# Softmax of a sparse graph-attention layer: exponentials per head with bias and accumulated sum on ScalarE

## The chip, the cores and the metric

The kernel runs on one core of one Trainium2 chip, as one launch. The metric is the device time of that launch in microseconds (us). A core has five engines, each with its own in-order queue: TensorE (PE, with its weight loads shown as PEld), VectorE (DVE), ScalarE (ACT), GpSimd (POOL) and SyncE (SP, which only starts transfers). They wait for each other through semaphores. Sixteen DMA engines are shared by all queues.

## The reference

One graph attention layer over 8192 nodes with 8 heads of width 32, in fp32. After a layer norm and a ReLU:

```python
h = (x @ W.T).reshape(n, H, D)                       # n=8192, H=8, D=32
s_src = einsum('nhd,hd->nh', h, a_src); s_dst = einsum('nhd,hd->nh', h, a_dst)
attn = s_src[:, None, :] + s_dst[None, :, :]
attn = attn + adj[:, :, None] * We[:, 0] + be
attn = where(adj > 0, attn, -inf)                    # only the edges count
attn = leaky_relu(attn, 0.2); attn = softmax(attn, axis=1)
out = einsum('ijh,jhd->ihd', attn, h) + x @ Wr.T + br + x0     # x0: the layer's input
```

`adj` is 8192 x 8192 fp32, some 268 MB, with few non-zero entries per row: most in the first rows, few in the last. So a row's softmax runs over its edges only.

## The kernel before

**Stages.** A prologue (to about 209 us) norms and projects all rows and writes a table of (h, s_dst) rows to HBM. The sparse stage then works through 63 tiles of 128 rows, and the epilogue (from about 2370 us) does tile 0, whose rows have too many edges, densely.

**Sparse stage, in two streams.** A *find* (`find`, `sort_step`, `decode`; sources c0 to c62, one tile of `adj` each) takes the edges out of a dense 128 x 8192 tile: DVE scans it with MAX8 (L615) and FIND_INDEX8 (L619) and sorts what it found in alternating steps. A *unit* (u0 to u62) is 128 rows with lists of at most K edges each. K falls from 75 (u0) over 36 (u7) and 22 (u10) to 6 (u62), with a rise at the start of each group of 8 tiles; within a group the rows are dealt out by their number of edges, so that rows of like length share a unit. For a unit:

- POOL gathers K table rows per partition, one indirect DMA for each (L493), into a ring of 86 slots.
- ACT makes the edge part of the scores in `prepare` (L932, 8 instructions, one for each head).
- DVE does the softmax in `softmax_step`, with its steps m = 0 to 6 between the sort steps of the find of that time: m=0 adds the gathered s_dst (L728), m=1 is the leaky ReLU (L732), m=2 the maximum of each head (L736), m=3 subtracts it (L739), m=5 sums the exponentials (L743), m=6 takes the reciprocal (L746).
- ACT takes the exponentials of all heads in one instruction (L942, `exps`), then weights the last 3 to 16 slots, 8 copies with a scale each (L947). DVE weights the others (`weight`, L755). PE adds the slots up with identity matmuls (L1079 for DVE's, L1085 for ACT's). DVE divides (`evacuate`, L765) one unit later, and POOL adds the result to `out` (L502) three units later.

**What orders it.** The queues are written out in Python. DVE's order for a unit is: the find, the sort steps with the softmax steps between, `weight`, `decode`, `evacuate` of the unit before. ACT's order is `prepare(u+1)`, `exps(u)` with its copies, `prepare(u+2)` and so on. `found[u]` says how many finds are done by unit u: 4, 7, 10, 12, 15, 16, 18, 20 for u0 to u7, then one for each unit until u50 does the last, c62.

SP loads the `adj` tiles (L394) into two buffers, eight pieces of 512 KB for each tile. The load of tile c waits for the scan of tile c-2 (semaphore `scanned`), and from tile 16 on each piece also waits until the piece before has landed, so that one piece at a time is under way.

For each of the groups there is a ranking: DVE counts (`count`, L685 to L696), PE sums in `ranks` (L1096 to L1103, queued behind `tile_sums` of the same unit, and so behind ACT's last copy of that unit), and DVE picks the ranks up one unit later in `place` (L705 to L715), which waits for PE. Then POOL deals the lists out (L512) before it goes on gathering. The rankings that matter below are those of u4 (picked up in u5), u10 (in u11) and u50 (in u51).

Of the kernel before, what the change touches and what calls it, by code (L numbers as in the profile page):

```python
# [15 lines left out]
ALU = mybir.AluOpType  # L16
ACT = mybir.ActivationFunctionType
# [3 lines left out]
AX_X = mybir.AxisListType.X  # L21

P = 128
N = 8192
IN = 256
H = 8
# [144 lines left out]
def gat_kernel(nc, x, adj, W, We, be, a_src, a_dst, Wr, br, out):  # L171
# [4 lines left out]
    with ExitStack() as ctx:  # L176
# [3 lines left out]
        def sb(name, shape, dt=F32):  # L180
            return ctx.enter_context(nc.sbuf_tensor(name, shape, dt))
# [66 lines left out]
        pre = sb("pre", [P, 2, KMAX * H])  # L248
        prob = sb("prob", [P, 2, KMAX * H])
        flag8 = sb("flag8", [P, 1])  # L250
        rmax = sb("rmax", [P, H])
        rsum = sb("rsum", [P, H])
        rinv = sb("rinv", [P, 2, H])
        w_flat = w_all[:, :, :].rearrange("p c n -> p (c n)")
        out_sb = w_flat[:, 0:OUTS * HD].rearrange("p (b n) -> p b n", n=HD)
# [6 lines left out]
        def part(width):  # L262
# [42 lines left out]
            "dec", "decoded", "pre_done", "flag_a", "flag_b",  # L305
            "headed", "validated", "counted", "compared", "above_summed", "rank_ps", "rank_picked", "rank_added", "ranked",
            "over_a", "over_b", "over_c",
            "landed0", "landed1", "landed2", "landed3", "z1", "z2", "z3", "z_ready", "exped", "summed_p", "recip",
            "weighted", "part_sum", "tile_sum", "evac",
            "fl_t", "fl_max", "fl_row", "fl_ready", "gr_ready", "act_weighted", "flag_init",  # L310
            "d_adj", "d_free", "d_mask", "d_ot", "d_oT", "d_dst0", "d_dst1", "d_w", "d_h0", "d_h1", "d_acc", "d_u1", "d_m1", "d_m2", "d_m", "d_leak", "d_own", "d_src", "d_exp",
# [19 lines left out]
        def landed(eng, seq):  # L331

            for lane in range(LANES):
                if seq > lane:
                    eng.wait_ge(S[f"landed{lane}"], 16 * ((seq - lane + LANES - 1) // LANES))
# [207 lines left out]
        def _(dve):  # L543
            v = nc.vector
# [173 lines left out]
            def softmax_step(un, m):  # L718

                u, K, b = un.u, un.K, un.u % 2  # L720
                z, pr = pre[:, b, 0:K * H], prob[:, b, 0:K * H]
                zv = z.rearrange("p (k h) -> p k h", h=H)
                zh, prh = (w.rearrange("p (k h) -> p h k", h=H) for w in (z, pr))
                if m == 0:
                    landed(dve, un.gather_seq + K)
                    dve.wait_ge(S["pre_done"], u + 1)
                    for k, at, n in un.slots(0, K):
                        last = v.tensor_tensor(zv[:, k:k + n, :], zv[:, k:k + n, :], gath[:, at:at + n, HD:ROW], ALU.add)  # L728
                    last.then_inc(S["z1"], 1)
                elif m == 1:  # L730
                    dve.wait_ge(S["z1"], u + 1)
                    v.scalar_tensor_tensor(out=z, in0=z, scalar=ALPHA, in1=z, op0=ALU.mult, op1=ALU.max  # L732
                                           ).then_inc(S["z2"], 1)
                elif m == 2:
                    dve.wait_ge(S["z2"], u + 1)
                    v.tensor_reduce(rmax[:, :], zh, AX_X, ALU.max).then_inc(S["z3"], 1)  # L736
                elif m == 3:
                    dve.wait_ge(S["z3"], u + 1)
                    v.tensor_tensor(zv, zv, rmax[:, :].unsqueeze(1).to_broadcast([P, K, H]), ALU.subtract  # L739
                                    ).then_inc(S["z_ready"], 1)  # L740
                elif m == 5:
                    dve.wait_ge(S["exped"], u + 1)
                    v.tensor_reduce(rsum[:, :], prh, AX_X, ALU.add).then_inc(S["summed_p"], 1)  # L743
                elif m == 6:
                    dve.wait_ge(S["summed_p"], u + 1)
                    v.reciprocal(rinv[:, b, :], rsum[:, :]).then_inc(S["recip"], 1)  # L746

            def weight(un):
# [136 lines left out]
        def _(act):  # L885
            s = nc.scalar
# [49 lines left out]
            def exps(un):  # L936

                u, K, b = un.u, un.K, un.u % 2
                act.wait_ge(S["z_ready"], u + 1)
                if u >= 2:  # L940
                    act.wait_ge(S["act_weighted"], units[u - 1].act_before)
                s.activation(prob[:, b, 0:K * H], pre[:, b, 0:K * H], ACT.Exp).then_inc(S["exped"], 1)  # L942
                act.wait_ge(S["exped"], u + 1)
                for k in range(K - un.act_slots, K):
                    for h in range(H):
                        g = gath[:, un.slot(k), h * D:(h + 1) * D]
                        last = s.activation(g, g, ACT.Copy, scale=prob[:, b, k * H + h:k * H + h + 1])  # L947
                    last.then_inc(S["act_weighted"], 1)

            prepare(units[0])  # L950
            for un in units:
                if un.u + 1 < len(units):
                    prepare(units[un.u + 1])
                exps(un)
# [248 lines left out]
```

## Time and profile before

| | us |
|---|---|
| median of 3 runs (2674.48 to 2684.55) | 2684.43 |
| the profiled execution, its own time | 2684.95 |
| span of that execution in the trace | 2683.3 |
| DVE busy | 2132.3 |
| POOL busy | 1485.7 |
| ACT busy | 1246.5 |
| PE busy | 1235.0 |

The profiled execution's own time is 1.65 us above its span, which is what lies around the trace. A row of the timeline gives the start, the duration, the engine, the line and the operation, the shapes, and in brackets how long the engine had sat idle before and what ended that. A row xN is N instructions that follow each other. The chain of waits is followed back from the last instruction, at each step to what released it. The granted TensorE clock is 0.681 of full speed on average.

### The profile page before, as it was taken

How to read it: one execution, taken by the hardware profiler on the slowest of the kernel's cores; microseconds unless marked ns; L12 is line 12 of the kernel's file. 1: busy time of each engine (PE TensorE's matmuls, PEld its weight loads, DVE VectorE, ACT ScalarE, POOL GpSimd, SP SyncE). 2: the span in 40 equal slices, each digit the busy share in tenths (PEclk: the TensorE clock that was granted, in tenths of full speed). 3: DMA queues.
4: the chain of work that ended last, by engine and by line, in shares of the span. 5: the costliest groups of instructions: out<-in, count | busy, mean ns of one | idle time of the engine just before them, and what ended most of it. 6: DMA issues, size and time to landing. Idle time of an engine off the chain costs nothing.

```text
span 2683.3 us, 27007 instructions
## 1 busy us (share of the span) xinstructions
PE 1235.0 (46%) x5305; PEld 934.2 (35%) x5306; DVE 2132.3 (79%) x4852; ACT 1246.5 (46%) x4898; POOL 1485.7 (55%) x1666
## 2 busy tenths in 40 slices
PE   6990022503334367446424524533341453518885
PEld 4660022402324245334322512422241342416664
DVE  3448959998998898999889988988997841259992
ACT  2320030221245498667546546444542655826662
POOL 5772656756675777777777476277347437710000
PEclk9995556757666676666666666666665666759998
DMA  3665656686676877877777677678668614477660
GB/s 114 195 228 191 216 131 195 167 249 178 179 226 192 225 240 225 245 229 243 229 224 239 199 233 222 183 231 233 208 193 234 200 39 100 95 225 173 157 156 3
DMA packets 226527, 512.79 MB, mean 191 GB/s; under 512 B 98280, under 2 KB 116400, under 8 KB 224208
## 3 DMA queue, kind: packets, MB, share of 16 engines
q1 hardware_dynamic: 151280, 319.60, 37.2%
q0 software_dynamic: 74960, 191.61, 28.1%
q14 instruction: 110, 0.90, 0.1%
q8 instruction: 33, 0.54, 0.1%
q10 hardware_dynamic: 144, 0.13, 0.0%
HBM read 475.19 MB, written 36.03 MB: 191 GB/s over the span
## 4 chain that ended last, share of the span: by engine, by line
DMA 56%; issue 18%; PE 10%; DVE 6%; POOL 6%; ACT 2%; SPq 1%; POOLq 0%; DVEq 0%; ACTq 0%; PEldq 0%
DMA adj_sb<-in_adj_dram 40%; DMA arena<-table,arena 8%; DMA arena<-table,own 6%; POOL arena L493 5%; PE banks L1058 2%; PE banks L1052 2%; ACT arena L947 1%; PE banks L1101 1%; DVE work L619 1%; PE banks L1079 1%; DVE work L615 1%; PE banks L1055 1%; PE banks L1154 1%; PE banks L1144 1%; DMA out_dram<-w_all,arena 1%
## 5 line engine op out<-in xcount | busy, mean ns | idle before, releaser
L493 POOL DMA_INDIRECT arena<-table,arena x943 | 972.6, 1031 | 354.5 <-issue 231.2
L1079 PE MATMUL banks<-arena,ident 128*128 128x256 f32 x1268 | 426.9, 513 | 1142.1 <-DVE arena L755 1142.1
L947 ACT ACTIVATE arena<-arena,prob 128x32 f32<-128x32 f32 x4024 | 859.5, 306 | 2.1
L1079 PEld LDWEIGHTS banks<-arena,ident 128*128 128x128 f32 x1268 | 332.6, 268 | 1234.8 <-issue 984.6
L615 DVE MAX8 work<-adj_sb 128x8 f32<-128x184 f32 (+51 forms) x624 | 580.9, 1005 | 116.0 <-DMA adj_sb<-in_adj_dram 115.5
L619 DVE FIND_INDEX8 work<-work,adj_sb 128x8 uint32<-128x184 f32 (+51 forms) x624 | 618.6, 1013 | 0.0
L942 ACT ACTIVATE prob<-pre 128x104 f32<-128x104 f32 (+26 forms) x63 | 20.3, 322 | 965.6 <-DVE pre L739 965.6
L1085 PE MATMUL banks<-arena,ident 128*128 128x256 f32 x1006 | 312.6, 442 | 106.3 <-ACT arena L947 106.2
L493 POOL DMA_INDIRECT arena<-table,own x194 | 202.2, 1042 | 157.4 <-DMA arena<-table,own 55.6
L1085 PEld LDWEIGHTS banks<-arena,ident 128*128 128x128 f32 x1006 | 197.3, 212 | 209.0 <-ACT arena L947 188.5
L932 ACT ACTIVATE pre<-arena,we_all 128x13 f32<-128x13 f32 (+23 forms) x480 | 146.5, 400 | 80.1 <-DMA arena<-lists 80.1
L755 DVE TENSOR_TENSOR arena<-arena,prob 128x768 f32<-128x768 f32 (+7 forms) x158 | 183.3, 1209 | 0.0
L502 POOL DMA_INDIRECT out_dram<-w_all,arena x60 | 99.7, 1662 | 147.3 <-DVE w_all L765 101.2
L728 DVE TENSOR_TENSOR pre<-pre,arena 128x80 f32<-128x80 f32 (+20 forms) x76 | 19.6, 271 | 165.9 <-DMA arena<-table,arena 131.8
L512 POOL DMA_INDIRECT lists<-arena,rank x60 | 59.7, 996 | 141.0 <-DVE rank L712 119.7
L1101 PE MATMUL banks<-work,ones 128*128 128x24 f32 (+6 forms) x404 | 89.1, 375 | 0.0
L1101 PEld LDWEIGHTS banks<-work,ones 128*128 128x128 f32 x404 | 85.6, 312 | 0.0
L1154 PE MATMUL banks<-ident,adj_sb 128*128 128x128 f32 x256 | 45.1, 308 | 62.4 <-ACT adj_sb L975 62.4
L1144 PE MATMUL banks<-pre,work 128*32 128x128 f32 x512 | 73.4, 290 | 0.0
L1058 PE MATMUL banks<-w_all,arena 128*128 128x256 f32 x256 | 72.4, 405 | 0.0
L1052 PE MATMUL banks<-w_all,arena 128*128 128x272 f32 x256 | 70.1, 397 | 0.0
L836 DVE TENSOR_TENSOR arena<-arena 128x4096 f32<-128x4096 f32 x16 | 70.0, 4419 | 0.0
(140 smaller groups left out, 1789.2 us busy)
## 6 DMA issues: line engine op xcount, KB each, us to landing
adj_sb<-in_adj_dram SPq DMA_DIRECT2D x504, 512.0 KB, 4.0
arena<-dst_rows SPq DMA_DIRECT2D x16, 2048.0 KB, 8.5
arena<-table,arena POOLq DMA_INDIRECT x943, 3.5
table<-arena POOLq DMA_DIRECT2D x32, 264.0 KB, 2.9
arena<-in_x_dram SPq DMA_DIRECT2D x32, 256.0 KB, 3.0
resid<-arena POOLq DMA_DIRECT2D x32, 256.0 KB, 2.6
out_dram<-arena POOLq DMA_DIRECT2D x32, 256.0 KB, 2.8
work<-table SPq DMA_DIRECT2D x8, 1024.0 KB, 10.9
```

Source lines behind the costliest of these rows:

```text
L493: pool.indirect_dma_start(gath[:, un.slot(k), :], None, table[:, :], bass.IndirectOffsetOnAxis(ap=rec[:, k, 0:1], axis=0), bounds_check=N ...
L615: last = v.max(val8[:, 8 * s:8 * s + 8], a[:, bounds[s]:bounds[s + 1]])
L619: last = v.max_index(idx8[:, 8 * s:8 * s + 8], val8[:, 8 * s:8 * s + 8], a[:, bounds[s]:bounds[s + 1]])
L755: last = v.tensor_tensor(gv, gv, pb.unsqueeze(3).to_broadcast([P, n, H, D]), ALU.mult)
L932: last = s.activation(pv[:, h, :], pairs(rec, K)[:, :, 1], ACT.Identity, scale=we_all[:, h:h + 1], bias=rec[:, 1 + h:2 + h])
L947: last = s.activation(g, g, ACT.Copy, scale=prob[:, b, k * H + h:k * H + h + 1])
L1052: m.matmul(ps_hd[:, q, b, :], rows, w_all[:, c, 0:272], start=(c == 0), stop=(c == 1))
L1058: last = m.matmul(ps_res[:, q, b, :], rows, w_all[:, c, 272:528], start=(c == 0), stop=(c == 1))
L1079: last = m.matmul(ps_sum[:, u % 2, :], ident[:, :], gath[:, un.slot(k), 0:HD], start=(k == 0), stop=False)
L1085: last = m.matmul(ps_sum[:, u % 2, :], ident[:, :], gath[:, un.slot(k), 0:HD], start=False, stop=(k == K - 1))
L1101: m.matmul(rv[:, i, :], ones[:, :], same[:, j * D:(j + 1) * D], start=False, stop=(i == n - 1 and j == i - 1))
L1144: last = m.matmul(ps_acc[:, b, :], hv[:, 4 * q + r, :], pt_sb[q % 4][:, r * P:(r + 1) * P], start=(q == 0 and r == 0), stop=(q == 15 and r ...
```

## The change

`rneg` (128 x 8) is new. Step m=3 no longer subtracts the maximum from all K x 8 scores: it negates the 8 maxima. ScalarE takes the exponentials head by head, with that head's negated maximum as bias (a pointer operand of one value for each partition) and with the sum over the head as accumulated output into `rsum`; the signal `exped` comes with the last head. Step m=5 (the sum) is gone with its semaphore, and the reciprocal at m=6 waits for `exped`.

```diff
@@ softmax_step
                 elif m == 3:
                     dve.wait_ge(S["z3"], u + 1)
-                    v.tensor_tensor(zv, zv, rmax[:, :].unsqueeze(1).to_broadcast([P, K, H]), ALU.subtract
-                                    ).then_inc(S["z_ready"], 1)
-                elif m == 5:
+                    v.tensor_scalar(rneg[:, :], rmax[:, :], -1.0, None, ALU.mult).then_inc(S["z_ready"], 1)
+                elif m == 6:
                     dve.wait_ge(S["exped"], u + 1)
-                    v.tensor_reduce(rsum[:, :], prh, AX_X, ALU.add).then_inc(S["summed_p"], 1)
-                elif m == 6:
-                    dve.wait_ge(S["summed_p"], u + 1)
                     v.reciprocal(rinv[:, b, :], rsum[:, :]).then_inc(S["recip"], 1)
@@ exps
-                s.activation(prob[:, b, 0:K * H], pre[:, b, 0:K * H], ACT.Exp).then_inc(S["exped"], 1)
+                ph, zh = (w[:, b, 0:K * H].rearrange("p (k h) -> p h k", h=H) for w in (prob, pre))
+                for h in range(H):
+                    last = s.activation(ph[:, h, :], zh[:, h, :], ACT.Exp, bias=rneg[:, h:h + 1], accum_out=rsum[:, h:h + 1])
+                last.then_inc(S["exped"], 1)
```

DVE's queue around the softmax of unit u50 (K = 11), before: the rows from the maximum to the first weighting; MAX and MATCH_REPLACE are the sort steps of find c62.

```order
L736 TENSOR_REDUCE rmax<-pre 128x8 [waits z2]
L651 MATCH_REPLACE work<-work 128x56 [waits sorted_]
L652 MATCH_REPLACE work<-work 128x56
L739 TENSOR_TENSOR pre<-pre,rmax 128x88 [waits z3]
L648 MAX work<-work 128x8 [waits sorted_]
L649 MAX work<-work 128x8
L654 TENSOR_SCALAR ahi<-work 128x20 [waits sorted_]
L743 TENSOR_REDUCE rsum<-prob 128x8 [waits exped]
L746 RECIPROCAL rinv<-rsum 128x8 [waits summed_p]
L755 TENSOR_TENSOR arena<-arena,prob 128x3x256 [waits exped]
```

The same place of the changed kernel (its line numbers differ by a few):

```order
L737 TENSOR_REDUCE rmax<-pre 128x8 [waits z2]
L652 MATCH_REPLACE work<-work 128x56 [waits sorted_]
L653 MATCH_REPLACE work<-work 128x56
L740 TENSOR_SCALAR rneg<-rmax 128x8 [waits z3]
L649 MAX work<-work 128x8 [waits sorted_]
L650 MAX work<-work 128x8
L655 TENSOR_SCALAR ahi<-work 128x20 [waits sorted_]
L743 RECIPROCAL rinv<-rsum 128x8 [waits exped]
L752 TENSOR_TENSOR arena<-arena,prob 128x3x256 [waits exped]
```

The subtraction over 88 columns has become an operation on 8, the sum is gone, and the reciprocal is now the first that waits for ScalarE.

ScalarE's queue at units u9 and u10 (K = 24 and 22), before:

```order
L942 ACTIVATE prob<-pre 128x192
L947 ACTIVATE arena<-arena,prob 128x32 x112
L932 ACTIVATE pre<-arena,we_all 128x20 x8
L942 ACTIVATE prob<-pre 128x176
L947 ACTIVATE arena<-arena,prob 128x32 x112
```

And now:

```order
L941 ACTIVATE prob,rsum<-pre,rneg 128x24 x8
L947 ACTIVATE arena<-arena,prob 128x32 x112
L929 ACTIVATE pre<-arena,we_all 128x20 x8
L941 ACTIVATE prob,rsum<-pre,rneg 128x22 x8
L947 ACTIVATE arena<-arena,prob 128x32 x112
```

One exponential of K x 8 columns has become eight of K columns; nothing else moved on this engine.

## Rows read from the trace of the kernel before

**Rows 1.** The page: the chain that ended last, share of the span by lines.
```profile
DMA adj_sb<-in_adj_dram 40%; DMA arena<-table,arena 8%; DMA arena<-table,own 6%; POOL arena L493 5%; PE banks L1058 2%; PE banks L1052 2%; ACT arena L947 1%; PE banks L1101 1%; DVE work L619 1%; PE banks L1079 1%; DVE work L615 1%; PE banks L1055 1%; PE banks L1154 1%; PE banks L1144 1%; DMA out_dram<-w_all,arena 1%
```

**Rows 2.** Who waited for whom: us in total, times, longest.
```profile
ACT prob L942 <- DVE pre L739: 965.6, 58, 99.2
...
DVE work L615 <- DMA adj_sb<-in_adj_dram: 115.5, 32, 9.0
...
DVE work L705 <- PE banks L1103: 25.3, 3, 9.6
...
DVE rsum L743 <- ACT prob L942: 22.2, 13, 8.3
```

**Rows 3.** The same view for SP's queue.
```profile
SPq L394 <- DMA adj_sb<-in_adj_dram: 1243.2, 336, 7.3
SPq L394 <- DVE work L619: 498.5, 17, 76.4
```

**Rows 4.** The chain of waits between 1100 and 2142 us, by lines.
```profile
by line: DMA adj_sb<-in_adj_dram 98.5%; SPq L394 1.1%; issue 0.6%
```

**Rows 5.** Groups of instructions: count, busy us, mean ns, idle us before.
```profile
L947 ACT ACTIVATE arena<-arena,prob 128x32 f32<-128x32 f32 x4024 | 859.5, 306 | 2.1
...
L743 DVE TENSOR_REDUCE rsum<-prob 128x8 f32<-128x104 f32 (+26 forms) x63 | 25.5, 405 | 22.2 <-ACT prob L942 22.2
...
L739 DVE TENSOR_TENSOR pre<-pre,rmax 128x104 f32<-128x104 f32 (+26 forms) x63 | 19.0, 301 | 0.4
```

**Rows 6.** Timeline of ACT in the dense epilogue, an exponential with accumulated sum.
```profile
2440.91 3.70 ACT L975 ACTIVATE arena<-arena,nmax 128x4096 f32<-128x4096 f32 x1
2444.51 0.19 ACT L975 ACTIVATION_READ_ACCUMULATOR arena<-arena,nmax 128x1 f32 x1
2444.60 0.25 ACT L980 ACTIVATE ot_sb<-banks 32x128 f32<-32x128 f32 x1
```

**Rows 7.** Timeline of ACT at unit u4 (K = 32).
```profile
770.97 0.42 ACT L942 ACTIVATE prob<-pre 128x256 f32<-128x256 f32 x1 [71.20 <-DVE pre L739]
771.42 27.23 ACT L947 ACTIVATE arena<-arena,prob 128x32 f32<-128x32 f32 x128
```

**Rows 8.** Timeline of DVE at unit u9 (K = 24).
```profile
983.92 0.35 DVE L739 TENSOR_TENSOR pre<-pre,rmax 128x192 f32<-128x192 f32 x1
...
985.68 0.18 DVE L746 RECIPROCAL rinv<-rsum 128x8 f32<-128x8 f32 x1
```

**Rows 9.** Timeline of ACT, the exponentials of u8, u9 and u10.
```profile
956.14 0.38 ACT L942 ACTIVATE prob<-pre 128x208 f32<-128x208 f32 x1 [0.56 <-DVE pre L739]
...
984.31 0.36 ACT L942 ACTIVATE prob<-pre 128x192 f32<-128x192 f32 x1 [1.53 <-DVE pre L739]
...
1011.91 0.35 ACT L942 ACTIVATE prob<-pre 128x176 f32<-128x176 f32 x1 [0.98 <-DVE pre L739]
```

**Rows 10.** The chain of waits around the load of tile c26: start, us, what.
```profile
1064.55 9.79 DVE work L619 x10
...
1074.36 3.77 DMA adj_sb<-in_adj_dram
```

**Rows 11.** Timeline of POOL, the first deal of the last group.
```profile
2192.63 1.02 POOL L512 DMA_INDIRECT lists<-arena,rank  x1 [19.29 <-DVE rank L712]
```

**Rows 12.** Timeline of ACT, the exponentials of u50, u56, u59, u60, u61 and u62.
```profile
2167.66 0.28 ACT L942 ACTIVATE prob<-pre 128x88 f32<-128x88 f32 x1 [14.79 <-DVE pre L739]
...
2285.41 0.27 ACT L942 ACTIVATE prob<-pre 128x104 f32<-128x104 f32 x1
...
2323.44 0.26 ACT L942 ACTIVATE prob<-pre 128x72 f32<-128x72 f32 x1 [3.02 <-DVE pre L739]
...
2336.16 0.26 ACT L942 ACTIVATE prob<-pre 128x64 f32<-128x64 f32 x1 [3.27 <-DVE pre L739]
...
2347.09 0.25 ACT L942 ACTIVATE prob<-pre 128x56 f32<-128x56 f32 x1 [1.50 <-DVE pre L739]
...
2357.89 0.24 ACT L942 ACTIVATE prob<-pre 128x48 f32<-128x48 f32 x1 [5.32 <-DVE pre L739]
```

More of the change, by code:

```diff
@@ L252, in gat_kernel @@
         rsum = sb("rsum", [P, H])
+        rneg = sb("rneg", [P, H])
         rinv = sb("rinv", [P, 2, H])
@@ L307, in gat_kernel @@
             "over_a", "over_b", "over_c",
-            "landed0", "landed1", "landed2", "landed3", "z1", "z2", "z3", "z_ready", "exped", "summed_p", "recip",
+            "landed0", "landed1", "landed2", "landed3", "z1", "z2", "z3", "z_ready", "exped", "recip",
             "weighted", "part_sum", "tile_sum", "evac",
@@ L720, in softmax_step @@
                 u, K, b = un.u, un.K, un.u % 2
-                z, pr = pre[:, b, 0:K * H], prob[:, b, 0:K * H]
+                z = pre[:, b, 0:K * H]
                 zv = z.rearrange("p (k h) -> p k h", h=H)
-                zh, prh = (w.rearrange("p (k h) -> p h k", h=H) for w in (z, pr))
+                zh = z.rearrange("p (k h) -> p h k", h=H)
                 if m == 0:
```

## The prediction

> **What bounds the kernel now.** I read four views, in this order. First the chain that ended last, by lines: the loads of the `adj` tiles are 40% of it, every compute line a few per cent [rows 1]. Then SP's waits: it waited 336 times for an `adj` piece to land (1243.2 us), but only 17 times for DVE's scan [rows 3]. Then the same chain between 1100 and 2142 us: 98.5% of it is `adj` pieces, one behind the other [rows 4]. So in that stretch, 1042 us long and u13 to u49 of the units, neither DVE nor ACT sets the time, although DVE is busy for 2132.3 us of the span. DVE itself waits for an `adj` tile 32 times, 115.5 us, 3.6 us each [rows 2]. Last the waits between the engines. ACT's exponentials waited 58 times for L739 (965.6 us), so ACT is mostly idle when they come. DVE waited only 22.2 us for them, because sort steps stand between. And three times DVE waited in L705 for PE's ranks (25.3 us) [rows 2], which themselves stand behind ACT's last copy of that unit. The reader should see that a change to the softmax is paid only where DVE or ACT is last: before tile c26 is loaded, and after c62 has been scanned.
>
> **What goes and what comes.** On DVE L739 (mean 0.30 us) and L743 (mean 0.41) go, 19.0 + 25.5 = 44.5 us in 63 units [rows 5]. A negation of 8 columns comes. The trace has none; the nearest row is the reciprocal of 8 columns, 0.18 us [rows 8], so 11 us. DVE's busy time falls by 33 us.
>
> On ACT one instruction becomes eight exponentials and eight reads of the accumulator. The nearest row to a short exponential with one pointer operand is the copy with a scale: 0.306 us for 32 columns [rows 5], and 128 of them take 27.23 us, 0.213 each from start to start [rows 7], so each begins 0.093 before the last one ends. 32 columns cost 0.027 of that: from 256 columns (0.42) to 88 (0.28) is 0.83 ns a column [rows 7, 12]. The read of the accumulator takes 0.19, starts 0.09 before its exponential ends, and the next instruction starts 0.09 after the read [rows 6]. A head of K columns is then 0.186 + 0.00083 K for the exponential and 0.095 for the read, and eight heads are 2.25 + 0.0066 K, plus 0.09 for the end of the last: 2.50 us for K = 24, 2.41 for K = 11. Bounds: if the reads cost nothing, 0.76 us less for a unit; if nothing overlaps, 0.49 a head, 1.6 us more. I take the overlapped value, since the epilogue's own pair of instructions shows it; its length there is another (4096 columns), which is why both bounds stay in the range.
>
> The cover: before, the exponential (0.3 to 0.4) ran under the two sort steps at m=4 and m=5. In u9, L739 begins at 983.92 and L746 at 985.68, 1.76 us later [rows 8]. Afterwards the reciprocal comes at 0.18 + 0.03 + 2.50 + 0.04 = 2.75: **DVE gets 1.0 us longer in this unit, not shorter**. With the shorter sorts of K < 16 it is 1.6 us longer. ACT's last head ends later by 2.50 - 0.36 - (0.35 - 0.18) = 1.97 us [rows 8, 9]. What is queued behind: on DVE `weight`, `decode` and the next find; on ACT the copies and with them PE's sums and ranks.
>
> **Where it counts.** I add up the delay along the chain.
>
> 1. Start to c16. The gathers of u0 to u3 end last there, not the softmax; u0 has so many sort steps that its sum goes for free (-0.2). u3 adds 0.3 on DVE. In u4 (K = 32) eight heads take 2.55 instead of 0.42, less 0.23 for the shorter step: +1.9. ACT's 128 copies follow without a pause [rows 7], then PE's ranks, then L705 in u5, where DVE waits (it is one of the three waits of rows 2). So the find of c16 is late by **2.0**, and its scan starts the load of c18.
>
> 2. c19 to c26. The loads carry the 2.0 to c19. u7 ends its heads 1.9 later: 3.9. Now ACT is nearly full: before the exponentials of u8, u9 and u10 it was idle for 0.56, 1.53 and 0.98 us only [rows 9], with 112 copies and eight `prepare` instructions between, and each unit adds 2.14. u8: 3.9 - 0.56 + 2.14 = 5.5. u9: the scores come later than ACT is free, 4.3, + 2.14 = 6.4. u10: 6.4 - 0.98 + 2.14 = 7.6. Behind u10's copies stand PE's ranks, behind these L705, the find of c24, and its scan ends at 1074.34, from where the load of c26 starts 0.02 later [rows 10]. Late by 7.6: **+5.6** in this step.
>
> 3. c26 to c62, 1074 to 2146 us: the loads follow each other [rows 4], and a find that is late by less than its wait costs nothing. DVE's growth of 1.0 to 1.6 us a unit stands against 3.6 us of wait a tile. Up to 1280 us the cover is thin, since there DVE hardly waits: in seven units it falls some 6 us further behind than the loads already are, and whether SP is by then still busy with the tile before is all that covers it. **0**, but this is the term most likely to be wrong upwards.
>
> 4. u50. Its exponentials (0.28 at 2167.66) are followed by copies, PE's ranks, L705, and POOL, which sat idle 19.29 us for this [rows 11, 12] and then paces the tail with its gathers: 2.41 - 0.28 - 0.06 = **+2.1**.
>
> 5. u55 to u62. POOL's gathers go on at their pace. ACT has no idle time before u56 [rows 12], nor before u57 and u58, and adds 2.15 in each: 2.0, 4.1, 6.3, 8.4. Then its idle 3.02, 3.27, 1.50 and 5.32 before u59 to u62 [rows 12] take some back: 8.4 - 3.0 + 2.1 = 7.5, 6.4, 7.0, and 7.0 - 5.3 + 2.1 = **3.8** for u62, whose copies, sum and store the epilogue waits for. The epilogue has none of the edited lines.
>
> Sum: 2.0 + 5.6 + 0 + 2.1 + 3.8 = 13.5 us. On the profiled execution (2684.95) that gives 2698.5. That execution lies 0.5 above the median of the runs, so the median should come to 2684.4 + 13.5 = 2698.0.
>
> **A rule of the skill.** The epilogue's rows give the read of the accumulator 0.19 us, of which 0.095 shows [rows 6]. The Trainium skill, "ScalarE: Activation LUTs", section "What ACT_TABLE_LOAD costs", prices an ACTIVATE with one pointer operand at 280 ns + 0.833 ns a column, with 93 ns of overlap back to back, and names no read at all; an estimate by that page alone makes eight heads 1.66 us for K = 11, and the sum about 3 us. The trace agrees with the page on the ACTIVATE and shows the read beside it.
>
> **The rivals.**
>
> - *The reads hide.* If an accumulator read runs wholly under the next exponential, a unit is 0.76 us shorter on ACT. Step 1 is then 1.0, step 2 about 0.5 (ACT stays below its idle time), steps 4 and 5 are 1.3 and 1.3, less 1 where DVE gains: about +3, 2687.5. Against it: L980 did wait for the read [rows 6]. 10%.
> - *The loads swallow step 2 as well*, because c25's pieces or SP's order leave more room than one execution shows: 2.0 + 2.1 + 3.8 = +8, 2692. For it: SP waited for a scan only 17 times. Against: c26 is one of these [rows 10]. 12%.
> - *Short instructions don't overlap with the read.* 1.6 us more a unit: steps 1 and 4 +1.6 each, step 2 +6, step 5 up to +12, and step 3 opens, since DVE's growth of 3 us a unit finds no cover in eight units before 1280 us, +24. About +59, 2743; with half of it +25, 2710. It decides from about 0.32 us a head. 14%.
> - *Faster: DVE is the bound and the cover suffices.* If eight heads took no longer than the sort steps (1.6 us and less), each unit on DVE's chain would save 0.30 + 0.41 - 0.18 = 0.53 us; about nine are on it (u3, u4, u7 to u11, u50, u62): -5, 2680. It needs under 0.18 us a head, and even the copies take 0.213 [rows 7]. 4%.
> - *The edit doesn't do what it says*, for instance a table load for each head: the instruction order shows one load of the table, before u0, as before, and no instruction beside the eight. Left out.
>
> **How the numbers follow.** The forecast (2693 to 2706, around 2698.0) has 60%. A measurement of this kernel can tell about 0.5%, 13.4 us, from no change: the limit is 2697.9, in the middle of my forecast. Of the 60% a little over half lies above, since what can go wrong in step 3 goes up; with the 14% that is 0.50 slower. Faster by more than 0.5% (below 2671) needs more than the rival gives; 0.03 for it and for the spread of the runs, of which one was at 2674.48. The rest, 0.47, is within. The range leaves out the lowest and the highest tenth: 2686 to 2714.
>
> **What the profile would show.** Right: eight exponentials and eight reads of a unit in 2.4 to 2.5 us; L746's successor waiting for ACT in nearly all units, over 50 us in all; DVE's busy time 33 us down and ACT's 130 up; the scan of c24 ending about 7.6 us later and that of c62 too; u62's heads ending 13.5 later. Wrong in step 3 if SP waits for scans between 1100 and 2142 us; wrong in step 2 if the scan of c24 moves by 2 or by 15; wrong in price if eight heads take 1.7 or 3.9 us.

## The result, and the profile after

The changed kernel takes **2700.77 us** (median of 9 runs, 2689.68 to 2703.26), the kernel before 2683.01 us beside it (9 runs, 2674.48 to 2691.09). The ratio is 1.0058, 95% interval 1.0038 to 1.0077: slower by 15 to 18 us, depending on whether the ratio or the two medians are taken. The profiled execution has a span of 2700.6 us, 17.3 more than before, at a granted clock of 0.680 (0.681 before).

The page of the changed kernel, busy time of each engine:

```profile
PE 1242.3 (46%) x5305; PEld 927.9 (34%) x5306; DVE 2106.1 (78%) x4789; ACT 1387.8 (51%) x5843; POOL 1483.3 (55%) x1666
```

DVE is busy for 26 us less than before, ACT for 141 us more. The groups of instructions of the changed kernel (count, busy us, mean ns, idle us before and what ended it) show from what:

```profile
L941 ACT ACTIVATE prob<-pre,rneg 128x13 f32<-128x13 f32 (+26 forms) x504 | 156.4, 313 | 845.6 <-DVE rneg L740 845.5
L941 ACT ACTIVATION_READ_ACCUMULATOR prob<-pre,rneg 128x1 f32 x504 | 94.1, 187 | 0.0
```
```profile
L743 DVE RECIPROCAL rinv<-rsum 128x8 f32<-128x8 f32 x63 | 12.8, 203 | 181.5 <-ACT prob L941 181.5
L740 DVE TENSOR_SCALAR rneg<-rmax 128x8 f32<-128x8 f32 x63 | 11.5, 183 | 0.4
```

504 exponentials and 504 reads of the accumulator stand where 63 exponentials stood. The negation costs what was assumed, 11.5 us. The last column of the reciprocal is the new thing: DVE waits for ACT in all 63 units, 181.5 us, where the sum had waited 22.2 us [rows 2]. Who waited for whom on DVE and on SP's queue, changed kernel (us in total, times, longest):

```profile
DVE rinv L743 <- ACT prob L941: 181.5, 63, 12.8
...
DVE work L616 <- DMA adj_sb<-in_adj_dram: 55.3, 20, 8.0
...
DVE work L706 <- PE banks L1103: 22.5, 3, 9.0
```
```profile
SPq L395 <- DMA adj_sb<-in_adj_dram: 1246.6, 336, 6.5
SPq L395 <- DVE work L620: 507.2, 17, 76.8
```

These answer rows 2 and 3. DVE's waits for an `adj` tile went from 115.5 us in 32 tiles to 55.3 us in 20: the 60 us that vanished there are what the longer units were paid with. SP still waits for a scan only 17 times, as before. And the chain of waits of the stretch in which the loads follow each other [rows 4] is as it was:

```profile
by line: DMA adj_sb<-in_adj_dram 98.7%; SPq L395 1.1%; issue 0.6%
```

The timeline of ACT at unit u9 (K = 24; start, duration, and in brackets the idle time before) shows the price of a head:

```profile
986.79 0.34 ACT L941 ACTIVATE prob<-pre,rneg 128x24 f32<-128x24 f32 x1 [0.36 <-DVE rneg L740]
987.03 0.19 ACT L941 ACTIVATION_READ_ACCUMULATOR prob<-pre,rneg 128x1 f32 x1
987.12 0.32 ACT L941 ACTIVATE prob<-pre,rneg 128x24 f32<-128x24 f32 x1
...
989.26 0.18 ACT L941 ACTIVATION_READ_ACCUMULATOR prob<-pre,rneg 128x1 f32 x1
989.48 1.17 ACT L947 ACTIVATE arena<-arena,prob 128x32 f32<-128x32 f32 x5
```

From one head to the next are 0.32 us, of which the read shows 0.09. From 986.79 to the end of the last read are 2.66 us; before, one instruction of 0.36 [rows 9]. DVE in the same unit:

```profile
986.54 0.22 DVE L740 TENSOR_SCALAR rneg<-rmax 128x8 f32<-128x8 f32 x1
...
989.48 0.20 DVE L743 RECIPROCAL rinv<-rsum 128x8 f32<-128x8 f32 x1 [1.52 <-ACT prob L941]
```

From this step to the reciprocal are 2.94 us against 1.76 [rows 8], and 1.52 of it is waiting. So DVE's unit is longer by 1.2 us although two of its instructions are gone.

Where the 17.3 us of the two traces lie, by events that both have:

| from | to | before | after | more | forecast |
|---|---|---|---|---|---|
| start | scan of c16 ends | 837.2 | 838.8 | 1.6 | 2.0 |
| start | scan of c24 ends | 1074.3 | 1080.3 | 5.9 | 7.6 |
| load of c26 issued | load of c62 issued | 1040.8 | 1045.0 | 4.2 | 0 |
| scan of c62 | heads of u50 end | 3.2 | 5.3 | 2.1 | 2.1 |
| first add of u53 | heads of u62 end | 142.2 | 145.9 | 3.8 | 3.8 |
| heads of u62 end | end | 325.2 | 327.6 | 2.4 | 0 |

These pieces don't cover the whole span; what lies between them (the end of c62's load and scan, u50 to u53) changed by -1.1 us together. The differences are taken before rounding.

### The profile page after: what moved, and what is told of

Same layout as the page of the kernel before. It is cut to its first block, busy times and chain, and to the rows that moved or that the text cites. A ratio compares the mean times of both kernels' runs of the same rounds, so it can differ in the third digit from the quotient of the medians.

```text
span 2700.6 us, 27889 instructions
## 1 busy us (share of the span) xinstructions
PE 1242.3 (46%) x5305; PEld 927.9 (34%) x5306; DVE 2106.1 (78%) x4789; ACT 1387.8 (51%) x5843; POOL 1483.3 (55%) x1666
## 4 chain that ended last, share of the span: by engine, by line
DMA 53%; issue 16%; PE 10%; DVE 9%; ACT 5%; POOL 5%; SPq 1%; POOLq 0%; DVEq 0%; ACTq 0%; PEldq 0%
DMA adj_sb<-in_adj_dram 40%; DMA arena<-table,arena 6%; DMA arena<-table,own 5%; POOL arena L494 4%; ACT arena L947 4%; DVE work L620 2%; PE banks L1058 2%; DVE work L616 2%; PE banks L1052 2%; PE banks L1101 1%; PE banks L1055 1%; PE banks L1154 1%; PE banks L1144 1%; ACT prob L941 1%; DVE adj_sb L822 1%
## 5 line engine op out<-in xcount | busy, mean ns | idle before, releaser
L1079 PEld LDWEIGHTS banks<-arena,ident 128*128 128x128 f32 x1268 | 323.3, 261 | 1214.3 <-issue 967.3
L616 DVE MAX8 work<-adj_sb 128x8 f32<-128x184 f32 (+51 forms) x624 | 580.9, 1006 | 56.1 <-DMA adj_sb<-in_adj_dram 55.3
L941 ACT ACTIVATE prob<-pre,rneg 128x13 f32<-128x13 f32 (+26 forms) x504 | 156.4, 313 | 845.6 <-DVE rneg L740 845.5
L494 POOL DMA_INDIRECT arena<-table,own x194 | 202.0, 1041 | 155.5 <-DMA arena<-table,own 55.3
L1085 PEld LDWEIGHTS banks<-arena,ident 128*128 128x128 f32 x1006 | 198.7, 217 | 249.7 <-ACT arena L947 230.2
L743 DVE RECIPROCAL rinv<-rsum 128x8 f32<-128x8 f32 x63 | 12.8, 203 | 181.5 <-ACT prob L941 181.5
L941 ACT ACTIVATION_READ_ACCUMULATOR prob<-pre,rneg 128x1 f32 x504 | 94.1, 187 | 0.0
```

Of the source, the lines that this page charges most:

```text
L494: pool.indirect_dma_start(gath[:, un.slot(k), :], None, table[:, :], bass.IndirectOffsetOnAxis(ap=rec[:, k, 0:1], axis=0), bounds_check=N ...
L616: last = v.max(val8[:, 8 * s:8 * s + 8], a[:, bounds[s]:bounds[s + 1]])
L941: last = s.activation(ph[:, h, :], zh[:, h, :], ACT.Exp, bias=rneg[:, h:h + 1], accum_out=rsum[:, h:h + 1])
L1079: last = m.matmul(ps_sum[:, u % 2, :], ident[:, :], gath[:, un.slot(k), 0:HD], start=(k == 0), stop=False)
L1085: last = m.matmul(ps_sum[:, u % 2, :], ident[:, :], gath[:, un.slot(k), 0:HD], start=False, stop=(k == K - 1))
```

## The experiments

Theory: the new instructions take ACT some 2.1 to 2.3 us more a unit, this counts only before c26 is loaded (part A) and after c62 is scanned (part B), and in between the loads of `adj` hide it (part C). The rivals that the prediction named lay in the price of a head (reads that hide, or heads that don't overlap), in the loads swallowing part A, and in DVE being the bound. Runs of one lot share the runs of the kernel before: its medians were 2689.67, 2688.03 and 2683.1 us in the three lots.

### One stretch of units at a time

The softmax of the changed kernel for some units, that of the kernel before for the others; both forms and both waits stand in the same program.

```diff
+        new = lambda u: u <= 12              # e1; e2: 13 <= u <= 49; e3: u >= 50
...
+                if new(u):
+                    for h in range(H):
+                        last = s.activation(ph[:, h, :], zh[:, h, :], ACT.Exp, bias=rneg[:, h:h + 1], accum_out=rsum[:, h:h + 1])
+                else:
+                    last = s.activation(prob[:, b, 0:K * H], pre[:, b, 0:K * H], ACT.Exp)
```

Expected of u0 to u12 alone:

> The change in u0 to u12 only; all other units as in the kernel before. My theory (the path runs through u4's copies, the ranks, c16, then u7 to u10, the ranks, c24, and SP then goes on from there): the whole early part of the sum stays, +6 to +8 us, and the scan of c24 ends 6 us later than before, as in the kernel after. Rival (the adj loads swallow it, since their chain has room): 0 to +2 us at the end, although DVE and ACT are as late in these units.

Expected of u13 to u49 alone:

> The change in u13 to u49 only, 37 of 63 units, in which it adds 1.0 to 1.6 us each to DVE and 2 us each to ACT. Theory (the loads of the adj tiles, one piece at a time, set the time there): 0 to +3 us; DVE's waits for adj tiles shrink from 115 us to some 55 us. Rival (DVE sets the time there after all): +37 to +60 us. Second rival (the softmax of this stretch slows the pieces themselves by contention, which would be the 4 us by which the load chain from c26 to c62 grew in the kernel after): +4 to +6 us, with the load chain from c26 to c62 at 1045 us and not 1041.

Expected of u50 to u62 alone:

> The change in u50 to u62 only. Theory: +2.1 us through u50's copies, the ranks and the deal, and +3.8 us through ACT, which has no idle time in u55 to u58: +6 us, with the heads of u62 ending 5.9 us later. Rival (POOL's gathers alone pace the tail): +2 us.

| changed units | median us | ratio, 95% | in us | forecast |
|---|---|---|---|---|
| u0 to u12 | 2698.07 | 1.0035 [1.0021, 1.0049] | +9.4 (5.6 to 13.2) | 7.6 |
| u13 to u49 | 2688.88 | 0.9998 [0.9982, 1.0014] | -0.5 (-4.8 to 3.8) | 0 |
| u50 to u62 | 2694.85 | 1.0022 [1.0007, 1.0037] | +5.9 (1.9 to 10.0) | 5.9 |

The three ratios add up to 0.55%, the whole change has 0.58%. **The loss is made in 26 of the 63 units, and the 37 in the middle cost nothing that these runs can show.** The intervals of the single rows are wide, though: 9.4 against 7.6 or against the +6 to +8 us expected is no difference that they can tell. The rival in which the loads swallow the second step asked for 2 us from the first row, and the row's interval begins at 5.6.

That the middle units are not cheap but covered is in DVE's waits of the second kernel (u13 to u49 changed):

```profile
DVE rinv L757 <- ACT prob L956: 74.6, 37, 3.3
DVE work L619 <- DMA adj_sb<-in_adj_dram: 56.5, 21, 9.1
```

and in those of the first (u0 to u12 changed):

```profile
DVE work L619 <- DMA adj_sb<-in_adj_dram: 116.1, 32, 8.0
```

In the middle DVE waits 74.6 us for ACT, 37 times, and in exchange 60 us less for `adj`. The tail is reproduced as closely: with u50 to u62 changed, first add of u53 to the last head of u62 takes 146.1 us, with the change in all units 145.9, with it in the others alone 142.6 and 142.5, before 142.2.

The same three traces say something about the 4.2 us of the middle stretch. From the load of c26 to that of c62 they have 1046.5, 1043.6 and 1050.4 us; the largest stands in the kernel in which none of these units is changed. So this length moves by some 10 us from one execution to the next without the edit, and the 4.2 us can't be put down to it.

### What of a head costs how much

First the kernel before with eight exponentials and nothing else: no bias, no accumulated sum, DVE subtracts and sums as before.

```diff
-                s.activation(prob[:, b, 0:K * H], pre[:, b, 0:K * H], ACT.Exp).then_inc(S["exped"], 1)
+                for h in range(H):
+                    last = s.activation(ph[:, h, :], zh[:, h, :], ACT.Exp)
+                last.then_inc(S["exped"], 1)
```

> The kernel before with its one exponential taken head by head in eight instructions; DVE still subtracts and sums, no bias operand, no accumulated sum. It separates the price of eight instructions from that of the pointer operand and the reads. Theory (fixed price by operand: about 0.11 us a head from start to start without a pointer and without a read): eight heads in 1.0 to 1.1 us, mostly under the sort steps, +2 to +4 us in all. Rival (an instruction of ScalarE costs 0.19 us a head whatever its operands): 1.6 us, +7 us.

Then the changed kernel without `accum_out`; DVE sums again at m=5.

```diff
-                    last = s.activation(ph[:, h, :], zh[:, h, :], ACT.Exp, bias=rneg[:, h:h + 1], accum_out=rsum[:, h:h + 1])
+                    last = s.activation(ph[:, h, :], zh[:, h, :], ACT.Exp, bias=rneg[:, h:h + 1])
```

> The changed kernel without the accumulated output: ScalarE still takes eight exponentials with the negated maximum as bias, VectorE sums them as before (behind the last head). It takes the eight reads of the accumulator away and gives DVE its 0.41 us sum back. Theory (a read shows 0.095 us): eight heads 0.76 us shorter than in the kernel after, 1.75 to 1.9 us; the stretch from the find of c19 to the end of c24's scan takes 3 to 4 us more than before (after: 6.3), the tail from the scores of u53 to the last head of u62 1 to 2 us more (after: 3.9); in all +7 us on before. Rival (the reads hide under the next exponential): both stretches as in the kernel after and +15 to +18 us.

The timeline of ACT at u9 (K = 24), the eight heads of the first kernel and of the second:

```profile
986.94 1.18 ACT L944 ACTIVATE prob<-pre 128x24 f32<-128x24 f32 x8 [1.25 <-DVE pre L739]
```
```profile
990.23 1.92 ACT L945 ACTIVATE prob<-pre,rneg 128x24 f32<-128x24 f32 x8 [1.06 <-DVE rneg L740]
```

| eight heads, us | K = 24 | K = 13 |
|---|---|---|
| one instruction (before) | 0.36 | 0.29 |
| eight exponentials | 1.18 | 1.02 |
| with the bias as pointer | 1.92 | 1.77 |
| with the read as well (after) | 2.66 | 2.51 |

So the price has three layers of nearly the same size: splitting 0.8 us, the bias 0.74 (0.093 an instruction), the read 0.74 (0.093). Rival "the reads hide" asked for 0.76 less than the forecast heads, that is 1.74 for K = 24; it is excluded. So is "short instructions don't overlap" with 3.9, and so is the rival of the first of these two kernels (0.19 us a head whatever the operands), which asked for 1.6 where 1.18 was measured.

The Trainium skill, "ScalarE: Activation LUTs", section "What ACT_TABLE_LOAD costs", adds about 93 ns for each pointer operand of an ACTIVATE: the two kernels agree with it, 0.093. It names no price for the read, which shows another 0.093 here.

In time: eight exponentials alone 2694.74 us, ratio 1.0025 [1.0007, 1.0043], +6.7 (1.9 to 11.6); with the bias 2699.94, 1.0039 [1.0026, 1.0053], +10.5 (7.0 to 14.2); the whole change about +15.6 by its ratio. Both medians lie above what was expected (+2 to +4, and +7), the first where its rival put it (+7). The time alone doesn't decide between the two; the eight heads do. The intervals overlap, but the order is that of the price, and the stretch from the find of c19 to the scan of c24, in which DVE waits for no load behind the first, has the same order, in us: 172.0 before, 174.6, 176.8, 178.2. The tail from the first add of u53 to the last head of u62 has 142.2, 142.3, 143.3 and 145.9.

### DVE's saving alone

The subtraction and the sum left out, the negation left in, one exponential as before; the softmax of this kernel is then not normalised, so it computes something else, and its time shows what DVE's saving is worth at most.

```diff
-                    v.tensor_tensor(zv, zv, rmax[:, :].unsqueeze(1).to_broadcast([P, K, H]), ALU.subtract
-                                    ).then_inc(S["z_ready"], 1)
-                elif m == 5:
-                    dve.wait_ge(S["exped"], u + 1)
-                    v.tensor_reduce(rsum[:, :], prh, AX_X, ALU.add).then_inc(S["summed_p"], 1)
+                    v.tensor_scalar(rsum[:, :], rmax[:, :], -1.0, None, ALU.mult).then_inc(S["z_ready"], 1)
```

> Only what VectorE is spared, at no price on ScalarE: the kernel before without the subtraction and without the sum (one exponential on the scores as they are, the negated maxima stand in the place of the sums). Its outputs are not the reference's. Theory (DVE is on the path only before c26, in u0 and from u50 on): -4 to -8 us although 44.5 us of DVE's work are gone; DVE's waits for adj tiles grow from 116 us to some 140 us. Rival (DVE, busy 79% of the span, is the bound): -30 to -40 us.

2683.8 against 2688.03 us, ratio 0.9982 [0.9968, 0.9996]: 4.8 us (1.1 to 8.6), within a few tenths of the prediction's rival "faster" (-5). DVE is busy for 2103.8 us, 28.5 less than before. Of that 11.9 us turn up as more waiting for `adj` (115.5 before; 140 had been expected), and 7.6 as more waiting for ACT's exponential, for which there are now fewer instructions in between (22.2 before):

```profile
DVE work L615 <- DMA adj_sb<-in_adj_dram: 127.4, 35, 9.4
...
DVE rinv L742 <- ACT prob L938: 29.8, 14, 8.9
```

An engine that is busy for 79% of the span gives back some 5 of 28 us, at most 9. That is the reading of rows 1 to 4, measured.

### Take the cover away: larger `adj` pieces

If the middle units are only hidden by the loads, quicker loads must bring their price to light. `PIECES = 4` makes four pieces of 1 MB out of eight of 512 KB, in the kernel before and in the changed one.

```diff
-PIECES = 8
+PIECES = 4
```

The kernel before with it:

> The kernel before with the adj tiles loaded in 4 pieces of 1 MB and not in 8 of 512 KB, still one piece at a time. Theory (from c26 to c62 the landings of the pieces in a row set the time, 29 us a tile for 8 pieces of 3.6 us; fewer pieces mean fewer times the fixed part of a landing): the chain from c26's to c62's load, 1041 us before, falls to 960 to 1000 us and DVE's waits for adj tiles fall under 30 us; -40 to -80 us. Rival (bandwidth, not the landing, sets a piece's time): within 10 us of before.

The changed kernel with it:

> The kernel after with the same 4 pieces. Theory: with the loads no longer last, DVE is, and its growth of 1.0 to 1.6 us in each of u13 to u49 comes on the path: +40 to +60 us against the same 4 pieces with the softmax of before, where with 8 pieces the difference was 18 us. Rival (the units of the middle cost nothing whatever the loads do): +15 to +20 us against it.

The kernel before falls to 2622.45 us, ratio 0.9733 [0.9707, 0.9758]; the changed one to 2678.02, 0.9961 [0.9949, 0.9974]. **The gap between the two softmaxes grows from some 16 us to 56 or 61** (2678.02 - 2622.45 gives 55.6, the ratios 2.28%; the two profiled executions are 45.7 apart). Why the loads are quicker, from the page's DMA issues (count, size, median us from issue to landing), first of the kernel before, then with four pieces:

```profile
adj_sb<-in_adj_dram SPq DMA_DIRECT2D x504, 512.0 KB, 4.0
```
```profile
adj_sb<-in_adj_dram SPq DMA_DIRECT2D x252, 1024.0 KB, 5.4
```

Twice the bytes cost 1.4 us more. If a piece costs a fixed part and a part in proportion to its bytes, which two sizes can't show, the fixed part is an estimated 2.6 us. SP waits for the piece before at 7 of the 8 pieces of a tile, and at 3 of 4: the first piece of a tile asks only for the scan, so it is issued while the last of the tile before is still under way, and two pieces are in flight there. That is why a tile of the kernel before took 1040.8 / 36 = 28.9 us in this stretch and not 8 x 4.0. SP's waits in the kernel before with four pieces:

```profile
SPq L394 <- DVE work L619: 1042.5, 61, 79.4
SPq L394 <- DMA adj_sb<-in_adj_dram: 743.1, 144, 7.9
```

The 144 waits for a piece are 3 in each of 48 tiles and take 743.1 us, where 336 (7 a tile) took 1243.2 [rows 3]. And now all 61 loads that can wait for a scan do so, against 17. DVE waits for `adj` in the middle no more, and is busy for 895.5 of the 950 us between 1100 and 2050, where it was 846.8. The chain of waits in this stretch has left the loads, but it is not DVE's alone; it goes back and forth between DVE and POOL's gathers (kernel before with four pieces):

```profile
by line: DMA arena<-table,arena 33.8%; issue 21.9%; POOL arena L493 11.1%; DVE work L619 7.0%; DVE work L615 6.6%; DMA out_dram<-w_all,arena 6.4%; DMA lists<-arena,rank 3.1%; ACT arena L947 1.8%; DVE arena L755 1.2%; POOL lists L512 1.0%; P
```

POOL in turn waits for DVE's ranks, the more the later DVE is; its waits in the same stretch, kernel before with four pieces, then the changed one:

```profile
POOL lists L512 <- DVE rank L712: 26.0, 2, 18.7
```
```profile
POOL lists L513 <- DVE rank L713: 63.3, 3, 26.6
```

DVE's waits between 1100 and 2050 us, kernel before with four pieces, then the changed one:

```profile
DVE pre L728 <- DMA arena<-table,arena: 40.0, 3, 18.7
DVE pre L728 <- issue: 5.8, 3, 4.0
DVE rsum L743 <- ACT prob L942: 1.3, 2, 0.8
```
```profile
DVE rinv L743 <- ACT prob L941: 70.9, 34, 3.6
DVE pre L729 <- DMA arena<-table,arena: 19.6, 1, 19.6
```

69.6 us more of waiting for ACT, 26 less for gathers (a later DVE finds them landed), some 15 less of work for as many units: 28 net; the stretch from the load of c26 to that of c62 grew by 35.5 (973.5 to 1009.0). So the mechanism is there, with its size to a fifth; the kernel with four pieces and the change in the middle alone, below, has 1011.2 us there. This is the stretch that the prediction priced at nothing and called most likely to be wrong upwards; it is nothing only as long as the tiles come as slowly as they do in eight pieces.

### Give DVE work to do while ACT takes the heads

Three kernels that look for a better version. First the change in u13 to u49 alone on four pieces; then the same with three of the next find's MAX8 (about 0.7 us each) put ahead of the reciprocal, where DVE stands idle.

```diff
+                    if m == 6 and new(un.u) and c is not None and c + 1 < len(sources):
+                        find_head(c + 1, 3)
                     softmax_step(un, m)
```

> 4 pieces for each adj tile, and the change in u13 to u49 only. With 8 pieces the same edit measured 0. Theory (with 4 pieces DVE, not the loads, sets the time of this stretch): 37 units of 1.0 to 1.4 us = +35 to +50 us against the kernel before with 4 pieces (2622 us), so 2655 to 2675. Rival (the 56 us between the two kernels with 4 pieces came from the ends, u0 to u12 and u50 on): +0 to +10 us, 2622 to 2632.

> As the kernel with 4 pieces and the change in u13 to u49, but VectorE takes the first three MAX8 of the next tile's find before the reciprocal, where it would wait for the eight heads; nothing else is moved or left out. Theory (the price of the change on DVE is the uncovered wait, 1.9 of 2.4 us): the wait goes to 0.1 to 0.3 us a unit, and each unit is then 0.3 to 0.5 us shorter than with the softmax of before: -10 to -20 us against the kernel before with 4 pieces, 2602 to 2612. Rival (ScalarE's longer work delays the sums and the gathers in another way): no better than 2650.

Without cover 2669.53 us, ratio 0.9947 [0.993, 0.9964]; with it 2628.15, 0.9784 [0.9752, 0.9816]. **The cover gives back 41 us of what the middle units cost on four pieces.** That cost is some 57 us by the ratios (0.9947 against 0.9733), which are of two lots. The traces have it in the stretch itself, from the scan of c24 to that of c62: 1023.8 us with the softmax of before, 1065.7 with the change in the middle units, 1025.0 with the cover, so that 40.7 of 41.9 us come back. This is the strongest evidence that the wait at the reciprocal, and not ACT's busy time as such, was the price: ACT does just as much in both. But it is no better than the softmax of before, where 10 to 20 us better had been expected; by its ratio (0.9784 against 0.9733, of two lots, with intervals that just meet) it may be worse. DVE's waits between 1100 and 2050 us in the kernel with cover say why:

```profile
DVE pre L743 <- DMA arena<-table,arena: 38.3, 3, 20.8
DVE rinv L768 <- ACT prob L969: 16.3, 21, 3.6
```

What DVE saves in 35 units there is 9.4 us of subtractions and 12.3 of sums less 6.3 of negations, 15.4 us; and the cover is too short in 21 units, which takes 16.3 us. In this stretch the two cancel. Whether a longer cover would gain anything is open: DVE waits 38.3 us for gathers there too, and the gathers and POOL's instructions that issue them are 51% of the chain of waits of this stretch.

Last, eight pieces for the 16 densest tiles and four after, with the softmax of before, and with the middle units changed and covered:

```diff
-PIECES = 8
+PIECES = lambda t: 8 if t < 16 else 4
```

> The kernel before with 8 pieces for the tiles up to 15, whose pieces do not wait for each other, and 4 from tile 16 on. With 4 pieces everywhere the scores of u3 came 12 us later than before (688.5 for 676.0 us), while the loads of that stretch are not on the path. Theory (bigger pieces in flight together slow the gathers of u0 to u3): 5 to 12 us better than 4 pieces everywhere, 2610 to 2618. Rival (that shift is the spread of the runs): 2618 to 2628.

> All together: 8 pieces up to tile 15 and 4 from there, the change in u13 to u49 with three MAX8 as its cover, and the softmax of before in the other units, where ScalarE is on the path. Theory: the sum of its parts, 15 to 30 us better than 4 pieces alone, 2592 to 2607. Rival (with DVE faster, POOL's gathers, 1.3 us each, become last in the middle): 2605 to 2622.

2613.59 us, ratio 0.9733 [0.9702, 0.9763], and 2615.95, 0.9746 [0.9711, 0.978]. By its ratio the first is not distinguishable from four pieces everywhere; that the early tiles like smaller pieces is therefore not shown. The second misses what was expected of it (2592 to 2607) and lies where its rival put it (2605 to 2622), whose reason the chain of waits between 1100 and 2050 us supports in part: gathers and the instructions that issue them are 49% of it, 41% with the softmax of before. The two kernels differ by less than their runs do. Both beat the kernel before by 2.5 to 2.7%: **what gains is the larger pieces; the change adds nothing to them, covered or not, and costs 56 us uncovered.**

## Why the prediction was right

**The sum.** Forecast 2698.0 us, measured 2700.77; +13.5 against +15.6 by the ratio (10.2 to 20.7) and +17.3 in the traces. What the traces have beyond the sum is 4.2 us in the load chain and 2.4 in the epilogue, both of which vary as much in kernels that don't touch them (the epilogue's last stretch had 324.0 to 327.6 us over all of them), less 1.7 by which steps 1 and 2 were too large and 1.1 between the pieces of the table. So where the loss is made, and by what, was right; that the total agrees to 2 or 4 us is in part luck, since the spread of these two stretches alone is larger.

**The price of a head.** Forecast 2.50 us for K = 24 and 2.41 for K = 11; measured 2.66, and 2.51 for K = 13. The overlap and the read (0.095 forecast, 0.093 measured) were right. The column was not: from K = 13 to 24 the eight heads grow by 0.15 us, 1.7 ns for each column of a head, twice the 0.83 taken from instructions with adjacent columns. A head's columns lie 8 elements apart, in what it reads and in what it writes. The writing alone is not it: the instructions of `prepare` also write 8 elements apart but read every second element, and eight of them take 2.42 us for K = 13 and 2.50 for K = 24, about 1 ns a column. That leaves the reading 8 apart as the likely cause, but no run changed it by itself. In u9 the heads were 0.16 us longer than forecast, which is most of the 1.2 us more on DVE instead of 1.0.

**Step 1** (start to c16, +2.0): 1.6. u4's heads ended 1.6 late, forecast 1.9.

**Step 2** (to the scan of c24, +5.6, in all 7.6): in all 5.9. Its entry was off, "The loads carry the 2.0 to c19. u7 ends its heads 1.9 later: 3.9". The find of c19 began at 902.04 instead of 902.28, and u7 ended 2.0 late. DVE's first scan instruction of c19, in the kernel before, in the changed one, and in the kernel with the change in u0 to u12:

```profile
902.28 9.17 DVE L615 MAX8 work<-adj_sb 128x8 f32<-128x101 f32 x9 [9.02 <-DMA adj_sb<-in_adj_dram]
```
```profile
902.04 9.17 DVE L616 MAX8 work<-adj_sb 128x8 f32<-128x101 f32 x9 [6.05 <-DMA adj_sb<-in_adj_dram]
```
```profile
905.87 9.17 DVE L619 MAX8 work<-adj_sb 128x8 f32<-128x101 f32 x9 [5.76 <-DMA adj_sb<-in_adj_dram]
```

The loads of c18 and c19 start with the end of the scan of c16 and do carry its delay, but how long they take varies: from that scan to the find of c19 were 65.1 us before, 63.3 in the changed kernel, 63.0 in the third, and 62.5 to 65.1 in the kernels that change other things. The kernel before stands at the long end, so 1.6 late became 0.2 early, and in the third kernel 5.7 late became 3.6. (Those 5.7 us are no measure of step 1: 4.1 of them were there in the heads of u3 beyond the changed kernel's, which has the same softmax up to there.) From the entry on the forecast adds 3.7 up to the scan of c24, and the trace 3.9: heads late by 2.0, 3.7, 4.8, 5.9 in u7 to u10, with ACT's idle time before u8, u9 and u10 down to 0.00, 0.36 and 0.00 from the 0.56, 1.53 and 0.98 of rows 9. The term left out is the spread of the loads, as large as the delay itself. The chain around the load of c26, changed kernel, answers rows 10:

```profile
1070.48 9.79 DVE work L620 x10
1080.28 0.02 issue
1080.29 3.68 DMA adj_sb<-in_adj_dram
```

**Step 3** (0): held, -0.5 us (-4.8 to 3.8) measured for the middle alone. With larger pieces it fails, +35.5 us, as the prediction's own condition (DVE's growth against 3.6 us of wait a tile) says.

**Step 4** (+2.1): u50's heads came 2.1 later after the scan of c62. The deal starts at 2204.20 instead of 2192.63 [rows 11], 11.6 later where the scan of c62 was 10.4 later, so 1.2 of it is left, and at the first add of u53 0.8, but 2.8 in the kernel that changes u50 to u62 alone. From the scan of c62 to that add were 51.3 us before, and 49.9 and 51.2 in the kernels with the change in other units only. The term is not contradicted, but no trace shows it to better than a microsecond or two. The deal in the changed kernel:

```profile
2204.20 1.02 POOL L513 DMA_INDIRECT lists<-arena,rank  x1 [18.75 <-DVE rank L713]
```

**Step 5** (+3.8, by way of 2.0, 4.1, 6.3, 8.4, 7.5, 6.4 and 7.0): this went as written. Less the 11.1 us by which u53 began late, the heads of u55 to u62 ended late by 2.1, 4.3, 6.5, 8.7, 7.7, 6.5, 7.1 and 3.8 us. In the timeline of ACT at u62, changed kernel, the 5.32 us of idle time of rows 12 are gone, for the copies of u61 end as the heads begin:

```profile
2367.70 3.06 ACT L947 ACTIVATE arena<-arena,prob 128x32 f32<-128x32 f32 x14
2370.66 0.29 ACT L941 ACTIVATE prob<-pre,rneg 128x6 f32<-128x6 f32 x1
```

**Busy times.** ACT +141 where 130 was forecast, some 7 of it by the columns; DVE -26 where -33 was forecast. The sum of what left and came is right by the durations (44.5 less 11.5), but busy time counts the overlap of two instructions once. Before, the reciprocal of u9 started at 985.68, 0.09 us before the sort step ahead of it ended; now it comes after a wait, and by an estimate from this unit such lost overlaps are 0.09 x 63 = 5.7 of the 7 us. The wait for ACT came to 181.5 us, "over 50" in the forecast: the bound was true and of little use, since the 1.3 to 3.3 us of each unit up to u49 and up to 12.8 in the backlog of the tail could have been added up.

## What to carry to other kernels

Before moving work from a busy engine to an idle one, ask in which stretch the busy engine is last: here DVE, busy for 79%, waited 3.6 us for a tile in 32 of them, so its saving was worth about 5 us, while the new work counted in full in the few units behind which ranks, deals and the epilogue wait. Folding a subtraction and a sum into an activation costs one instruction for each head, each with a pointer operand and a read of the accumulator, and rows as short as these (K of 6 to 36 in most units) don't pay that back. And where the chain of waits is 98% serial transfers, their size is the first thing to try: doubling it was worth 66 to 72 us, four times what the change lost.

## What the runs showed of the hardware that was not expected

- A read of the accumulator behind a short exponential takes 187 ns and shows 93; a bias by pointer shows 93; eight bare exponentials of 13 columns take 1.02 us, 0.13 each.
- A short exponential whose columns lie 8 elements apart, read and written, costs 1.7 to 1.8 ns a column (K = 24 against 13), with bias and read or without; one over adjacent columns 0.83 [rows 7, 12]; a copy with scale and bias that reads 2 apart and writes 8 apart about 1. That the distance of the reads is the cause was not tested by itself.
- A piece of 512 KB lands in 4.0 us (median) and one of 1 MB in 5.4, so by the estimate above 2.6 us of each don't scale with size; SP's mean wait for a piece, 3.7 and 5.2 us, gives 2.2. The Trainium skill, "DMA: Bandwidth & Descriptors", section "Latency and other measured facts", speaks of a fixed cost of about 2 us, mostly the latency of the memory; the runs are near it, 2.2 to 2.6.
- The same load chain of 36 tiles (load of c26 to load of c62) took between 1037 and 1050 us in kernels that load the same bytes in the same order, more than most of the terms of this case. A term of 4 us in such a stretch can't be read from a pair of traces; it takes many runs.
